# Layer 1 of a field-interaction kernel as three fp32r products, with new turns for row sums, gathers and splits

## The reference

```python
x0 = xk = tables[feat, sparse]                   # (512, 26, 32)
for w, bb in ((conv1_w, conv1_b), (conv2_w, conv2_b)):
    hp = einsum('bhd,bmd->bhmd', xk, x0)         # all products of two rows
    xn = sigmoid(einsum('oi,bid->bod', w, hp) + bb)
    xk, r = xn[:, :64], xn[:, 64:]
    res.append(r)
cin = concat(res).sum(-1) @ cin_w + cin_b
h1 = tanh(concat(emb, dense) @ W1 + b1)          # 845 -> 1024
h2 = tanh(h1 @ W2 + b2)                          # -> 512
h3 = tanh(h2 @ W3 + b3)                          # -> 256
out = linear + cin + h3 @ deep_w + deep_b + bias
```

## Time and profile before

| | us |
|---|---|
| median of 3 runs (426.15 to 427.26) | 426.61 |
| the profiled execution | 427.28 |
| its span, first to last instruction | 425.2 |
| TensorE busy | 406.2 (96%) |
| VectorE busy | 312.3 (73%) |
| GpSimd busy | 166.6 (39%) |
| ScalarE busy | 160.9 (38%) |

### The profile page before, as it was taken

How to read it: one execution, slowest core, us unless ns; L and a number is a source line. 1 busy time by engine, 2 the same in 40 slices (tenths; PEclk the granted TensorE clock), 3 DMA queues, 4 the chain that set the end, 5 groups by cost and what they waited for, 6 DMA issues and landing times.

```text
span 425.2 us, 5237 instructions
## 1 busy us (share of the span) xinstructions
PE 406.2 (96%) x1850; PEld 164.2 (39%) x1850; DVE 312.3 (73%) x345; ACT 160.9 (38%) x269; POOL 166.6 (39%) x148
## 2 busy tenths in 40 slices
PE   3968999989999999999999999999999989999997
PEld 1322333323333333333333333333333326887885
DVE  4006977979989889898989898988989893732223
ACT  3054343435444435436262534443543601111112
POOL 6752662463643735645748340000000371870000
PEclk9996999999999999999999999999999999999999
DMA  5458679998999999999899999988876940330000
GB/s 200 84 119 184 162 168 226 228 228 216 227 239 236 237 226 231 232 223 237 212 233 221 229 211 229 216 207 205 208 193 163 224 115 0 102 98 2 0 0 1
DMA packets 42176, 74.12 MB, mean 174 GB/s; under 512 B 20593, under 2 KB 23025, under 8 KB 42150
## 3 DMA queue, kind: packets, MB, share of 16 engines
q1 hardware_dynamic: 38566, 72.03, 71.1%
q0 software_dynamic: 3584, 1.76, 3.1%
HBM read 72.06 MB, written 1.71 MB: 173 GB/s over the span
## 4 chain that ended last, share of the span: by engine, by line
PE 77%; DMA 8%; POOL 6%; DVE 4%; issue 3%; SPq 2%; DVEq 0%
PE conv L479 36%; PE conv L457 16%; PE conv L500 8%; PE ring L500 7%; POOL emb L372 6%; PE ring L469 5%; DMA emb<-in_table,rows 4%; PE ring L439 4%; DMA copied<-laid 4%; DVE copied L800 2%; SPq L318 1%; DVE prod L800 1%; PE ring L514 1%; DMA idx_sb<-in_idx 0%; SPq L307 0%
## 5 line engine op out<-in xcount | busy, mean ns | idle before, releaser
L372 POOL DMA_INDIRECT emb<-in_table,rows x112 | 133.9, 1196 | 114.8 <-DMA emb<-in_table,rows 83.1
L800 DVE TENSOR_TENSOR copied<-copied,xk 128x1024 f32<-128x1024 f32 x112 | 134.0, 1226 | 5.4 <-DMA copied<-laid 5.2
L800 DVE TENSOR_TENSOR prod<-ring,xk 128x1024 f32<-128x1024 f32 x96 | 115.4, 1220 | 30.2 <-PE ring L469 28.3
L479 PE MATMUL conv<-copied,w_sb 128*64 128x512 f32 x448 | 105.9, 594 | 3.9 <-DVE copied L800 3.7
L479 PE MATMUL conv<-prod,w_sb 128*64 128x512 f32 x384 | 98.5, 619 | 1.1 <-DVE prod L800 1.1
L631 ACT ACTIVATE xk<-conv,const_sb 64x512 f32<-64x512 f32 x64 | 43.6, 682 | 128.9 <-PE conv L457 128.0
L457 PE MATMUL conv<-sq,w_sb 117*64 117x512 f32 x384 | 88.1, 593 | 0.3 <-ACT sq L660 0.3
L620 ACT ACTIVATE sq<-ring 117x512 f32<-117x512 f32 x90 | 48.6, 594 | 27.3 <-PE ring L439 25.2
L479 PEld LDWEIGHTS conv<-copied,w_sb 128*64 128x64 f32 x448 | 31.2, 137 | 69.5 <-issue 46.2
L457 PEld LDWEIGHTS conv<-sq,w_sb 117*64 117x64 f32 x384 | 27.2, 136 | 54.2 <-issue 54.0
L381 POOL TENSOR_TENSOR xt_lo<-xt,xt_hi 128x480 fp32r<-128x480 f32 (+1 forms) x7 | 9.4, 1366 | 88.7 <-ACT xt_hi L695 84.1
(11 more groups left out here) (98 smaller groups left out, 298.7 us busy)
## 6 DMA issues: line engine op xcount, KB each, us to landing
copied<-laid SPq DMA_DIRECT2D x224, 256.0 KB, 5.5
wpiece<-in_mlp SPq DMA_DIRECT2D x22, 256.0 KB
raw<-laid SPq DMA_DIRECT2D x64, 52.0 KB
emb<-in_table,rows POOLq DMA_INDIRECT x112
laid<-emb SPq DMA_DIRECT2D x16, 96.0 KB
sel_f<-in_sel SPq DMA_DIRECT2D x1, 832.0 KB, 6.1
const_sb<-in_const SPq DMA_DIRECT2D x1, 626.5 KB, 4.5
w_sb<-in_w SPq DMA_DIRECT2D x1, 416.0 KB, 6.6
```

The costliest lines, as they stand in the source:

```text
L372: pool.indirect_dma_start(out=emb[0:n, i, j, :], out_offset=None, in_=table, in_offset=bass.IndirectOffsetOnAxis(ap=rows[0:n, i, j:j + 1], ...
L479: mm = nc.tensor.matmul(conv[i % 2][c * HALF:(c + 1) * HALF, :], w2_sb[:, t, :], prod_of(r)[:, c, :], start=(t == 0), stop=(t == T2 - 1))
L800: nc.vector.tensor_tensor(prod_of(r)[:, :, :].rearrange("p c n -> p (c n)"), left[:, :, :].rearrange("p c n -> p (c n)"), xk[i % 2][:, :, ...
```

## The change

Five things change.

Layer 1 of pairs 2 to 15 is three fp32r products (high weight by high square, low weight by high square, high weight by low square) on the whole array of 128 output columns, nine matmuls a half instead of six fp32 ones. ScalarE makes the high parts of the squares, GpSimd five of the six low parts of a pair and VectorE the sixth.

The row sums of pair i + 2 stand one by one ahead of the spreads of groups 0, 1 and 2 of pair i, so x of pair i + 2 is wanted when pair i begins. `x_low(i + 3)` therefore stands behind tile 11 of pair i, where `x_low(i + 2)` stood behind tile 5. `fetch(i + 3)` stands ahead of the fourth copy.

GpSimd's gathers of pair i + 4 are no longer one run from start to end. They wait for the products of pair i and stand in turns with the low squares.

For pairs 0 and 1 the rows go from `emb` to a free copy buffer (`wide`) inside SBUF, without `laid` and `raw`.

The first deep tile is cut into three parts, behind groups 0, 1 and 2 of pair 15. Five of seven input slices of W1 are split late (`late_copy`, `late_low`, `late_high`), ten pieces, in the room of the squares; the folds and the transpose of the last pair are moved.

The diff, cut to its core (the tables, GpSimd's, SP's, TensorE's, ScalarE's and VectorE's parts in this order):

```diff
+DIRECT = 2
...
-LAY_AT, FETCH_AT = 1, 4
-DEEP_AT = 2
+LAY_AT, FETCH_AT = 1, 3
+DEEP_IN = {0: (0, 1), 1: (2, 3), 2: (4, 5, 6)}
 GROUPS = ((0, 1, 2, 3), (4, 5, 6, 7), (8, 9, 10, 11), (12,))
 SPREADS_IN = (((0, 4),), ((0, 8), (0, 9)), ((0, 12), (1, 0)), ((1, 1),))
-SUMS_IN = {0: ((1, 2),), 2: ((2, 0),), 3: ((2, 1),)}
+SUMS_IN = ({1: 0, 2: 1, 3: 2}, {0: 0, 1: 1, 2: 2})
 L1_IN = {0: 0, 1: 1}
-X_LOW_AT, TURN_AT, FOLD1_AT, PIECE_AT = (10, 5), 9, (5, 5), 11
+TURN_AT, FOLD1_AT, PIECE_AT = 9, (5, 5), 11
+KEEP = 2
+LOW_AT, LATE_AT = 2, 10
...
+        def wait_rows(eng, i):
+
+            if i < DIRECT:
+                for j in range(GJ):
+                    eng.wait_ge(early_in[i][j], 16)
+            else:
+                eng.wait_ge(rows_in[i % GSEM], ROWS * (i // GSEM + (1 if i % GSEM >= DIRECT else 0)))
...
+            where = SUMS_IN[min(i, 2) - 1]
+            return [(i + 2, where[g])] if g in where and i + 2 < NPAIR else []
...
+            def direct(i):
+
+                for j in range(GJ):
+                    m = GM if j < NG else ML
+                    sp.wait_ge(early_in[i][j], 16)
+                    sp.dma_start(wide[i][j * GM:j * GM + m, :, :].rearrange("p c n -> p (c n)"),
+                                 emb[0:m * PB, i, j, 0:E]).then_inc(wide_in[i], 16)
...
+            direct(0)
             lay_out(0)
-            fetch(0)
             for n in range(2):
                 copy(n)
+            direct(1)
             lay_out(1)
-            fetch(1)
             for n in range(2, RC):
                 copy(n)
             lay_out(2)
...
-            def gather(i):
-
-                if i >= GSEM:
-                    pool.wait_ge(rows_in[i % GSEM], ROWS * (i // GSEM))
-                if i >= 2:
-                    pool.wait_ge(rows_in[(i - 1) % GSEM], ROWS * ((i - 1) // GSEM + 1))
-                for j in range(GJ):
+            def gather(i, parts=range(GJ)):
+
+                for j in parts:
+                    if j == 0 and i >= 2:
+                        wait_rows(pool, i - 1)
                     n = P if j < NG else ML * PB
                     pool.indirect_dma_start(
                         out=emb[0:n, i, j, :], out_offset=None, in_=table,
                         in_offset=bass.IndirectOffsetOnAxis(ap=rows[0:n, i, j:j + 1], axis=0),
-                    ).then_inc(rows_in[i % GSEM], 16)
+                    ).then_inc(early_in[i][j] if i < DIRECT else rows_in[i % GSEM], 16)
+
+            def sq_low(i, u, c):
+
+                pool.wait_ge(sq_hi_done, highs_up_to(i, u, c))
+                nc.gpsimd.tensor_tensor(sq_lo[i % 2][0:UK, u, c, :], sq[i % 2][0:UK, u, c, :],
+                                        sq_hi[i % 2][0:UK, u, c, :].bitcast(F32), ALU.subtract)\
+                  .then_inc(sq_lo_done, 1)
...
+            for i in range(GSEM):
+                gather(i)
             for i in range(NPAIR):
-                gather(i)
-
-            pool.wait_ge(prod_done, T2 * (NPAIR - 2) + 12)
-            for k in range(3):
-                xt_low(k)
-            pool.wait_ge(prod_done, T2 * (NPAIR - 1) + 4)
-            for k in range(3, 5):
-                xt_low(k)
-            pool.wait_ge(prod_done, T2 * (NPAIR - 1) + 8)
-            for k in range(5, K1):
-                xt_low(k)
-            xt_low_rest()
+                ahead = i + GSEM < NPAIR
+
+                pool.wait_ge(prod_done, T2 * i + 4)
+                if 2 <= i + 1 < NPAIR:
+                    sq_low(i + 1, 2, 1)
+                if i == NPAIR - 2:
+                    late_low(0)
+                if i == NPAIR - 1:
+                    xt_low(2)
+                    xt_low(3)
+                if ahead:
+                    gather(i + GSEM, range(0, 2))
+
+                pool.wait_ge(prod_done, T2 * i + 8)
+                if 1 <= i and i + 2 < NPAIR:
+                    sq_low(i + 2, 0, 0)
+                    sq_low(i + 2, 0, 1)
+                if i == NPAIR - 2:
+                    late_low(1)
+                    late_low(2)
+                if i == NPAIR - 1:
+                    for k in range(4, K1):
+                        xt_low(k)
+                if ahead:
+                    gather(i + GSEM, range(2, 4))
+
+                pool.wait_ge(prod_done, T2 * i + 12)
+                if i == 0:
+                    sq_low(2, 0, 0)
+                    sq_low(2, 0, 1)
+                if i + 2 < NPAIR:
+                    sq_low(i + 2, 1, 0)
+                    sq_low(i + 2, 1, 1)
+                if i == NPAIR - 2:
+                    xt_low(0)
+                    xt_low(1)
+                if ahead:
+                    gather(i + GSEM, range(4, GJ))
...
+                if i < 2:
+                    for u in range(UT):
+                        pe.wait_ge(sq_done, squares_up_to(i, u, c))
+                        for q in range(2):
+                            o = slice(q * HALF, (q + 1) * HALF)
+                            mm = nc.tensor.matmul(bank[o, :], w1a_sb[:, u, o], sq[i][0:UK, u, c, :],
+                                                  start=(u == 0), stop=(u == UT - 1))
+                    mm.then_inc(l1_done, 1)
+                    return
                 for u in range(UT):
-                    pe.wait_ge(sq_done, squares_up_to(i, u, c))
-                    for q in range(2):
-                        o = slice(q * HALF, (q + 1) * HALF)
-                        mm = nc.tensor.matmul(l1_bank(i, c)[o, :], w1_sb[:, u, o], sq[i % 2][0:UK, u, c, :],
-                                              start=(u == 0), stop=(u == UT - 1))
+                    pe.wait_ge(sq_hi_done, highs_up_to(i, u, c))
+                    nc.tensor.matmul(bank[:, :], w1_hi[:, u, :], sq_hi[i % 2][0:UK, u, c, :],
+                                     start=(u == 0), stop=False)
+                    nc.tensor.matmul(bank[:, :], w1_lo[:, u, :], sq_hi[i % 2][0:UK, u, c, :],
+                                     start=False, stop=False)
+                for u in range(UT):
+                    if (u, c) in LOWS:
+                        pe.wait_ge(sq_lo_done, lows_up_to(i, u, c))
+                    else:
+                        pe.wait_ge(sq_lo_dve, i - 1)
+                    mm = nc.tensor.matmul(bank[:, :], w1_hi[:, u, :], sq_lo[i % 2][0:UK, u, c, :],
+                                          start=False, stop=(u == UT - 1))
...
+            slot_free("sums", 1, 0)
+            for k in range(2):
+                nc.tensor.matmul(sums_bank(1, 0)[:, 0, :], w2_sb[:, 0:2, :].rearrange("p t o -> p (t o)"),
+                                 w2_sb[:, 0:8, :].rearrange("p t o -> p (t o)"), start=True, stop=True)
...
-                    if i == NPAIR - 1 and g == DEEP_AT:
-                        pe.wait_ge(piece_lo, KW)
-                        pe.wait_ge(l2_read, NPAIR - 1)
-                        deep(0, 0)
+                    if i == NPAIR - 1 and g in DEEP_IN:
+                        if g == 0:
+                            pe.wait_ge(piece_lo, KW)
+                            pe.wait_ge(l2_read, NPAIR - 1)
+                        deep(0, 0, DEEP_IN[g])
...
+                if i < DIRECT:
+                    act.wait_ge(wide_in[i], 16 * GJ)
+                    act.wait_ge(zeroed, 2 + i)
+                    for c in range(2):
+                        nc.scalar.activation(x[i][HALF * c:HALF * c + M, :], wide[i][0:M, c, :], ACT.Copy, scale=-1.0)\
+                          .then_inc(x_hi_done, 1)
+                    return
+                act.wait_ge(raw_in[i % RX], raw_landed(i))
...
+                if i == 1:
+                    x_high(3)
                 sigmoid2(i - 1)
-                if i + 1 < NPAIR:
-                    squares(i + 1, 2)
-                if i + 2 < NPAIR:
-                    x_high(i + 2)
+                if i > 1:
+                    squares(i + 2, 0)
+                    square_highs(i + 2, 0)
                 if i <= KW:
                     piece_high(i - 1)
+                if i == NPAIR - 2:
+                    act.wait_ge(l1_done, 2 * (NPAIR - 1))
+                    for m in range(NL):
+                        late_copy(m)
                 if i + 1 < NPAIR:
                     sigmoid(i + 1, 0)
+                squares(i + 2, 1 if i > 1 else 0)
+                square_highs(i + 2, 1 if i > 1 else 0)
+                squares(i + 2, 2 if i > 1 else 1)
+                if i + 1 < NPAIR:
                     sigmoid(i + 1, 1)
-                if i + 2 < NPAIR:
-                    squares(i + 2, 0)
-                    squares(i + 2, 1)
+                if i + 3 < NPAIR:
+                    x_high(i + 3)
+                square_highs(i + 2, 2 if i > 1 else 1)
...
-                    if t == X_LOW_AT[k] and i + 2 < NPAIR:
-                        x_low(i + 2)
-                    if t == FOLD1_AT[k]:
+                    if i == 0 and t == 10:
+                        x_low(2)
+                    if i == 1 and t == 2:
+                        x_low(3)
```

(14 more changed lines are left out.)

178 lines of the change are left out of this document (134 added, 44 removed).

## The result

The changed kernel took 458.59 us (median of 4 runs, 457.81 to 459.49) against 426.88 us before: a ratio of 1.0739, 95% interval 1.0708 to 1.0771. That is 23.5 us slower than the 435.1 forecast and above the range of 414 to 448.

A forecast was written before the change was run, and what follows sets the result against it. TensorE sets the pace before; GpSimd's 20.4 us turn was to bound the changed kernel. Turns +11.1, pairs 13 and 14 -1.2, pair 15 -1.4: +8.5 us on 427.28, 435.8, median 435.1 us; range 414 to 448.

The forecast's parts named there:

- TensorE's part: Layer 1 on TensorE: 2.29 us a half instead of 2.58, so an even pair takes 19.2 us (bounds 18.7 to 19.2).
- the cost of the mode: TensorE going from 64-column matmuls to whole-array ones and back in Layer 1: 0.24 us a half.
- GpSimd's part, "the term that decides": GpSimd's turn per pair: seven gathers 10.2, four low squares 5.7, landing 4.5, together 20.4 us, longer than TensorE's 19.2.
- the sign that I named: In the profile after, GpSimd waiting for products would show the forecast wrong and GpSimd's turn fitting within 19.2 us.
- rival A: GpSimd's turn fits in 19.2 us or less; only the first +5.9 us stays; median 421.9 us; chance 0.20.
- rival B: GpSimd's turn is below 18 us and gates nothing; 19.2 us a pair; median 413.0 us; chance 0.14.
- How this reaches the end: From gather landing through laid, raw and x to the mains: 10.8 us; GpSimd's turns delay pairs, +8.5 us in all.
- rival C: SP's list is the bound, a ring through main, laid, raw and x: 19.8 us a pair; 428.5 us; chance 0.12.
- VectorE's part: VectorE near 17.7 us a pair plus 1.0 us for GpSimd's five low squares: 18.7 us, just under TensorE.
- The direct rows: Start of pairs 0 and 1: pair 0 comes 2 to 4 us earlier, lost again as pair 2 waits for gather 4.
- The end: Pair 15 with the split first deep tile gains 1.4 us, 0 if late pieces come late; the deep network 0.
- D: Rival: GpSimd's turn is 21.8 us, as with gathers of 11.6 us; 450.5 us; chance 0.12.

The follow-up runs named there:

- e14: Changed kernel with x high ahead of sigmoids, x low after tile 12, earlier gathers, layout first in SyncE's turn, but Layer 1 wholly fp32, no square splits: ratio 1.0034.
- e17: Changed kernel with x high and x lows moved, gathers and layout earlier, half 1 of Layer 1 fp32, GpSimd's low square held until x low is made: ratio 1.0019.
- e15: Changed kernel with its own order of turns, but Layer 1 wholly in fp32 and no high or low squares: ratio 1.0618.
- e7: Changed kernel with x high ahead of the sigmoids, x low after tile 12, and gathers, layout and fetch earlier: ratio 1.0289.
- e4: Changed kernel with GpSimd's five low squares a pair left out, the third term reading the high squares instead: ratio 1.0584.
- r5: The changed kernel as it stands, run a second time: ratio 1.0690.

## Why the prediction was wrong

That it is slower was right, the mechanism and so the size were not.

- **TensorE's part: right.** Halves of Layer 1 take 2.25 and 2.27 us (priced 2.29). The stretch without x is 18.97 us, in the bounds of 18.7 to 19.2. Layer 1 of one half in three terms is worth 19.78 - 19.50 = 0.28 us a pair (e14 and e17, TensorE busy throughout in both); 0.29 was priced, the cost of the mode included.
- **GpSimd's part, "the term that decides": this step failed.** The gathers were priced well: 137.8 us busy and 25.3 of issue over 112 are 1.46 us each. The low squares took 1.28 us instead of 1.43. What was wrong is the 4.5 us of landing added to the turn. The gathers of the next turn stand behind tile 3 and a low square, by when the last ones have mostly landed: in pairs 6 to 12 only 2.1 us of idle time in all end on a landing. GpSimd's turn in pairs 6 to 11 is 16.9 us of work, issue gaps included, 0.4 us of landing and 4.1 us of waiting for products, not 20.4 us of work and landing. By the sign that I named this is rival A, and by the length of the turn, below 18 us, even rival B; but their 19.2 us a pair never came, as another ring was there.
- **How this reaches the end: right place, wrong cause.** VectorE is idle ahead of x low behind tile 11, released by ScalarE, as forecast. I followed x high only back to `raw` and not back along ScalarE's own list, where the squares of group 2 and the sigmoids of half 1 stand ahead of it. That these wait for TensorE's half 1 of the same pair closes a ring of 21.36 us. Its path could be read from the engines' lists in the diff. e15 shows that the turns alone make it: 21.53 us a pair with no square split. One of the next two obstacles was the one I had in rival C: with x high moved, it waited for `raw`. The other was x low beside low squares, which I had at nothing.
- **VectorE's part: mis-sized.** 1.0 us a pair was taken for GpSimd's five low squares. It is 2.4 us in the pairs of e7, where VectorE has no idle time (1.55 against 1.21 us, seven times), and 0.2 us in the changed kernel, where the ring leaves the low squares room: in e4 their removal left the period at 21.36. Rows 9 against 5 already gave 0.54 us for a pair of products; I argued it down.
- **The early pairs: missed.** Pair 2 opened at 94.4 us (forecast 86.0). Pair 1 took 28.9 us for 20.6. Of two executions that both began late, the one without splits opens pair 2 at 89.4 us (e15), 5.0 earlier; of two that both began early, the one without GpSimd's low squares opens it at 87.0 instead of 90.2 (e4 against r5). So the splits cost about 5 us here and GpSimd's low squares 3 of them; what the other 2 are isn't separated. I priced the low squares only as part of GpSimd's turn. In pairs 2 to 4 the ring is longer still, 23.0 to 23.5 us in e15. In pair 4 of e15 all of the 2.0 us lie between x low and Layer 1: 0.7 is the weight piece of VectorE between x low and tile 12, and 1.3 is TensorE, whose granted clock was 0.51 from 135.8 to 139.2 us, its lower level, after a wait of 2.0 us for products. (In the changed kernel's own execution it was 0.50 in pair 1 too, from 71.6 to 75.0 us, after 3.7 us of idle time.) The mains behind it in that pair, and the same in pair 9 at the full clock:

```profile
135.64 3.62 PE L591 MATMUL conv<-prod,w_sb 128*64 128x512 f32 x8
...
245.31 1.94 PE L591 MATMUL conv<-prod,w_sb 128*64 128x512 f32 x8
```

- **The direct rows: right in size.** A start 2.5 us earlier (32.1 for 34.6 us in the second run). It is gone by pair 1 already (61.1 for 59.5), so it isn't gather 4 that takes it back, as I had it.
- **The end: right, if low.** Pair 15 gained 2.1 us (1.4 forecast); the deep network 0.
- **A slip in the sums of the rivals.** A and D keep the forecast's 86.0 us for pair 2, though their first turn is 1.2 us shorter and 1.4 us longer: A should be 420.7 us and D 451.9.

Where the 30.7 us of the profiled execution lie, then: pair 2 opens 14.3 us late, of which 4.2 are the odd start (94.4 against 90.2 us in the second run), 5.0 the splits, and 5.1 not separated. Pairs 2 to 4 lose 5.6 us and pairs 5 to 12 lose 13.2, where the new turns without any split lose 8.9 and 14.0 (e15). The last pairs win 2.4.

## What to carry to other kernels

When an instruction is moved, write down what stands ahead of it and behind it in every engine's list that it passes through, and follow each of these until the chain leaves or comes back: if it comes back within one iteration, its sum is a lower bound of the period, whatever the engines' busy times are. A period that repeats to a few hundredths while no engine is full points to such a ring. Behind it the next limit may be near (here 0.4 us lower), so an edit of one wait is to be judged by the new period, not by the wait that it removed, and its instructions are to be timed again in their new places: x low met other neighbours there. Work given to an engine that is idle isn't free if its operands share the memory of the engine that is full.
